# Attention products as plain fp32 on both row halves of TensorE, in place of split fp32r parts on 128 rows

## The reference

```
xn  = (x - mean(x)) * rsqrt(var(x) + eps) * gamma + beta        # per sample
q   = Wq @ xn + bq ;  k, v = Wkv @ ctx + bkv                    # 8 heads x 64 channels
att = softmax((q * scale)^T (k * scale))                        # 256 x 256 per head
out = x + Wo @ (att @ v^T)^T + bo
```

## Time and profile before

| | |
|---|---|
| runs, median | 944.0 us (944.0 and 944.01) |
| profiled execution | 944.01 us, the slower of the two; its span from first to last instruction is 941.7 us |
| PE matmul busy | 919.0 us, 98% |
| PE weight load | 691.6 us, 73% |
| DVE | 810.3 us, 86% |
| ACT | 758.3 us, 81% |
| POOL | 671.0 us, 71% |
| DMA | 93.32 MB, mean 99 GB/s |

### The profile page before, as it was taken

The page is one execution under the profiler, slowest core; times in us unless marked ns, Lnnn a source line. Parts: engine busy times, 40 slices in busy tenths (PEclk is TensorE's granted clock), DMA queues, the critical chain, the costliest instruction groups (busy, mean ns, idle before and its releaser), DMA issues.

```text
span 941.7 us, 25082 instructions
## 1 busy us (share of the span) xinstructions
PE 919.0 (98%) x6852; PEld 691.6 (73%) x6852; DVE 810.3 (86%) x1899; ACT 758.3 (81%) x2569; POOL 671.0 (71%) x648
## 2 busy tenths in 40 slices
PE   5999999999999999999999999999999999999998
PEld 4777777777777777777777777777777777777775
DVE  5888889888889888898888898888898888898885
ACT  2788888788888878887888887888888888888785
POOL 2667777667787667877777776677776677777674
PEclk9999999999999999999999999999999999999999
DMA  6444444444444344444444444434444444433431
GB/s 120 100 107 95 114 100 100 96 106 93 107 110 95 91 109 100 95 117 94 95 100 106 100 105 97 104 89 115 103 100 93 106 96 103 114 90 83 96 82 36
DMA packets 72741, 93.32 MB, mean 99 GB/s; under 512 B 15316, under 2 KB 39892, under 8 KB 72724
## 3 DMA queue, kind: packets, MB, share of 16 engines
q1 hardware_dynamic: 70800, 92.72, 42.6%
q10 hardware_dynamic: 1924, 0.40, 0.3%
HBM read 21.76 MB, written 4.19 MB: 28 GB/s over the span
## 4 chain that ended last, share of the span: by engine, by line
PE 53%; DVE 24%; issue 13%; ACT 9%; DMA 0%; DVEq 0%; ACTq 0%; SPq 0%; POOL 0%
PE turned L488 15%; PE out_bank L502 14%; ACT probs L595 8%; PE fill L457 7%; PE fill L458 7%; DVE xhat L722 5%; DVE neg_max L676 5%; DVE probs_t L671 4%; PE misc L518 3%; PE misc L519 3%; DVE c_straight L730 2%; DVE c_crossed L731 2%; PE fill L463 2%; PE fill L464 2%; DVE t_low L687 2%
## 5 line engine op out<-in xcount | busy, mean ns | idle before, releaser
L788 POOL TENSOR_TENSOR probs<-probs,recip 128x512 f32<-128x512 f32 x512 | 526.6, 1055 | 155.6 <-DVE recip L682 150.0
L595 ACT ACTIVATE probs<-fill,neg_max 128x256 f32<-128x256 f32 x1024 | 475.4, 484 | 82.5 <-DVE neg_max L676 82.5
L676 DVE TENSOR_REDUCE neg_max<-fill 128x2 f32<-128x512 f32 x512 | 347.9, 680 | 65.4 <-PE fill L458 60.7
L488 PE MATMUL turned<-ident,probs 128*128 128x128 f32 x2048 | 325.5, 282 | 6.2 <-DVE probs_t L671 6.2
L457 PE MATMUL fill<-c_straight,t_stack 128*128 128x256 f32 x1024 | 308.9, 324 | 0.5 <-DMA t_stack<-t_low 0.5
L488 PEld LDWEIGHTS turned<-ident,probs 128*128 128x128 f32 x2048 | 224.0, 142 | 114.9 <-issue 62.6
L502 PE MATMUL out_bank<-probs_t,values 128*64 128x256 f32 x2048 | 277.5, 392 | 1.4 <-ACT probs_t L586 1.4
L458 PE MATMUL fill<-c_crossed,t_stack 128*128 128x256 f32 x1024 | 265.2, 280 | 0.0
L595 ACT ACTIVATION_READ_ACCUMULATOR probs<-fill,neg_max 128x1 f32 x1024 | 218.8, 214 | 0.0
L586 ACT COPY probs_t<-turned 128x512 f32<-128x512 f32 x256 | 150.1, 586 | 78.2 <-PE turned L488 77.9
L502 PEld LDWEIGHTS out_bank<-probs_t,values 128*64 128x64 f32 x2048 | 124.4, 136 | 105.7 <-issue 34.8
(11 more groups left out here) (61 smaller groups left out, 547.7 us busy)
## 6 DMA issues: line engine op xcount, KB each, us to landing
t_stack<-t_up SPq DMA_DIRECT2D x256, 128.0 KB, 2.3
t_stack<-t_low SPq DMA_DIRECT2D x256, 128.0 KB, 2.3
x<-in_x SPq DMA_DIRECT2D x64, 128.0 KB, 2.7
c<-in_ctx SPq DMA_DIRECT2D x64, 128.0 KB, 2.7
x_res<-in_x SPq DMA_DIRECT2D x32, 128.0 KB, 2.1
out<-y SPq DMA_DIRECT2D x32, 128.0 KB, 1.7
wq<-in_L_xattn_Wq ACTq DMA_DIRECT2D x2, 128.0 KB
wv<-in_L_xattn_Wkv SPq DMA_DIRECT2D x2, 128.0 KB
```

Source lines behind the costliest of these rows:

```text
L488: mm = pe.transpose(turned[unit % PT_BANKS][:, S * kt + 128 * qt:S * kt + 128 * qt + 128], probs[:, unit % PROBS, qt, 128 * kt:128 * kt + ...
L595: ins = act.activation(probs[:, unit % PROBS, qt, :], bank[:, K * qt:K * qt + K], ACT.Exp, bias=neg_max[:, unit, qt:qt + 1], accum_out=den ...
L676: dve.tensor_reduce(neg_max[:, unit, :], fill[bank_of("scores", unit)][:, :].rearrange("p (t k) -> p t k", t=QT), AX.X, ALU.max, negate=Tr ...
L788: pool.tensor_tensor(p, p, recip[:, unit, :].unsqueeze(2).broadcast_to([128, QT, K]), ALU.mult).then_inc(probs_ready, 1)
```

## The change

The three split products become plain fp32 products with 64 rows, issued two at a time: one on rows 0 to 63 and one on rows 64 to 127 of the array, each into a bank of its own. Nothing is split any more: `t_up`, `t_low`, `t_stack`, `x_stack`, `c_straight`, `c_crossed`, their casts and subtractions and the sixteen stacking DMAs of a pair are gone. Weights, xhat and ctx already lie on both halves.

- A score **step** now makes two units, the even and the odd head of one sample; 8 steps a pair. A projection makes four heads (2 a pair, the banks read by ACT as `t_even` and by DVE as `t_odd`), a values item one half of the keys of both samples (2 a pair, one ACT copy of 1024 columns).
- The `fill` banks are now two **bank pairs**. Values use them too, so `FILLS` has 12 items, and each waits for the readers of the item two places earlier.
- An attend covers two heads, 4 a pair. Unit order is now sample-major within a head pair.
- All positions are new.

```diff
-FILL_BANKS = 4
+FILL_PAIRS = 2
-PROJ, VALUES, DISTANCE = -8.57, -4.16, 1.87
-PE_ORDER = (every("scores", -3.69, UNITS) + every("proj", PROJ, HP, 4) + every("turn", 1.26, UNITS)
-            + every("attend", 4.1, H, PS) + every("values", VALUES, PS * KT, DISTANCE)
+STEPS = UNITS // 2
+SCORES, PROJ, VALUES = -3.7, -8.5, -5.6
+PE_ORDER = (every("scores", SCORES, STEPS, 2) + [(PROJ, "proj", 0), (PROJ + 4.9, "proj", 1)] + every("turn", 1.26, UNITS)
+            + every("attend", 6.1, HP, 4) + every("values", VALUES, KT, 4)
             + [(-13.42, "mean", 0), (-11.99, "var", 0)])
-ACT_ORDER = (every("t_hi", PROJ + 0.21, HP, 4) + every("exp", -2.39, UNITS)
+ACT_ORDER = ([(PROJ + 0.4, "t_even", 0), (PROJ + 5.4, "t_even", 1)] + every("exp", -2.39, UNITS)
              + [work for work in every("copy", 1.27, UNITS) if work[2] not in DVE_EVACS]
-             + every("values", VALUES + 0.38, PS * KT, DISTANCE))
-DVE_ORDER = (every("t_lo", PROJ + 1.08, HP, 4) + every("max", -3.24, UNITS) + every("recip", -1.98, UNITS)
+             + [(VALUES + 1.1, "values", 0), (VALUES + 5.0, "values", 1)])
+DVE_ORDER = ([(PROJ + 0.6, "t_odd", 0), (PROJ + 5.6, "t_odd", 1)] + every("max", -3.24, UNITS) + every("recip", -1.98, UNITS)
              + [work for work in every("copy", 0.93, UNITS) if work[2] in DVE_EVACS]
              + [(-15.75, "moments", 0), (-14.01, "mean_var", 0), (-13.2, "spread", 0),
-                (-12.47, "sample_var", 0), (-11.46, "norm", 0), (-7.73, "c_hi", 0), (18.63, "result", 0)])
+                (-12.47, "sample_var", 0), (-11.46, "norm", 0), (20.63, "result", 0)])
...
-FILLS = [(_kind, _item, _at) for _at, _kind, _item in in_order(PE_ORDER) if _kind in ("scores", "proj")]
+FILLS = [(_kind, _item, _at) for _at, _kind, _item in in_order(PE_ORDER) if _kind in ("scores", "proj", "values")]
...
+            def free_banks(pair, k):
+                for back in range(FILL_PAIRS, NFILL + 1, FILL_PAIRS):
+                    kind, item, step = FILLS[(k - back) % NFILL]
+                    owner = pair.shift(-(back > k) - int(step // UNITS))
+                    if owner.exists():
+                        if kind == "scores":
+                            wait(pe, exp_ready, owner.count(UNITS, 2 * item + 2))
+                        elif kind == "proj":
+                            wait(pe, t_even_ready, owner.count(HP // 2, item + 1))
+                            wait(pe, t_odd_ready, owner.count(HP // 2, item + 1))
+                        else:
+                            wait(pe, values_ready, owner.count(KT, item + 1))
+                        break
+
+            def scores(pair, step, banks):
+                hp, s, p = step // PS, step % PS, pair.parity()
                 for qt in range(QT):
-                    lhs = t_stack[:, h, s, 128 * qt:128 * qt + 128]
-                    dst = bank[:, K * qt:K * qt + K]
-                    pe.matmul(dst, lhs, c_straight[p][:, s, :], start=True, stop=False)
-                    mm = pe.matmul(dst, lhs, c_crossed[p][:, s, :], start=False, stop=True)
+                    for o in range(2):
+                        r = 64 * o
+                        mm = pe.matmul(banks[:, o, K * qt:K * qt + K], t[r:r + 64, hp, s, 128 * qt:128 * qt + 128],
+                                       c2[p][r:r + 64, s, :], start=True, stop=True)
                 mm.then_inc(scored, 1)
...
+            def project(pair, i, banks):
+                for o in range(2):
+                    r = 64 * o
+                    hp = 2 * i + o
+                    mm = pe.matmul(banks[:, o, :], qk_gamma[r:r + 64, 2 * hp:2 * hp + 2, :],
+                                   xhat[pair.parity()][r:r + 64, :, :], start=True, stop=True)
+                mm.then_inc(projected, 1)
+
+            def make_values(pair, kt, banks):
+                for s in range(PS):
+                    r = 64 * s
+                    mm = pe.matmul(banks[:, s, :], c2[pair.parity()][r:r + 64, s, 128 * kt:128 * kt + 128],
+                                   u_t[r:r + 64, :, :], start=True, stop=True)
+                mm.then_inc(values_summed, 1)
...
-            def attend(pair, h):
+            def attend(pair, hp):
...
+                if hp == 0:
+                    wait(pe, values_ready, pair.count(KT, KT))
                     wait(pe, y_ready, pair.count(1, 0))
+                for h in (2 * hp, 2 * hp + 1):
+                    for kt in range(KT):
+                        for s in range(PS):
+                            mm = pe.matmul(out_bank[64 * s:64 * s + 64, 0:S], values[pair.parity()][:, s, kt, h, :],
+                                           probs_t[:, unit_of(h, s) % PROBS_T, kt, :],
+                                           start=(h == 0 and kt == 0), stop=(h == H - 1 and kt == KT - 1))
...
             def exponentials(pair, unit):
-                bank = fill[bank_of("scores", unit)]
+                bank = fill[banks_of("scores", unit // 2)][:, unit % 2, :]
...
+            def copy_values(pair, kt):
+                wait(act, values_summed, pair.count(KT, kt + 1))
...
+                act.copy(values[pair.parity()][:, :, kt, :, :], fill[banks_of("values", kt)][:, :, :]
+                         ).then_inc(values_ready, 1)
```

More of the change, by code:

```diff
@@ L246, in build @@
         y = [sb(f"y_{i}", [128, S]) for i in range(2)]
-        fill = [pb(f"fill_{i}", [128, 512]) for i in range(FILL_BANKS)]
+        fill = [pb(f"fill_{i}", [128, 2, 512]) for i in range(FILL_PAIRS)]
         turned = [pb(f"turned_{i}", [128, 512]) for i in range(PT_BANKS)]
@@ L437, in output_value_products @@
                 mm.then_inc(w_mm, 1)
[L439 to L450, removed]
@@ L467, in fill_bank, with fill_banks @@
+            def make_values(pair, kt, banks):
[4 more added lines that the diff above has]
+                mm.then_inc(values_summed, 1)
+            def fill_banks(pair, kind, item, owner):
                 k = fill_of(kind, item)
-                free_bank(pair, k)
+                free_banks(pair, k)
+                banks = fill[k % FILL_PAIRS]
@@ L469, in fill_bank @@
                 if kind == "scores":
+                    if item % (2 * PS) == 0:
+                        wait(pe, t_even_ready, owner.count(HP // 2, item // (2 * PS) + 1))
+                        wait(pe, t_odd_ready, owner.count(HP // 2, item // (2 * PS) + 1))
+                    scores(owner, item, banks)
+                elif kind == "proj":
                     if item == 0:
[L471 to L473 removed]
@@ L474, in fill_bank @@
-                    scores(owner, item, fill[k % FILL_BANKS])
+                        wait(pe, xhat_ready, owner.count(2, 2))
+                    project(owner, item, banks)
                 else:
                     if item == 0:
-                        wait(pe, x_stack_ready, owner.count(1, 1))
-                    project(owner, item, fill[k % FILL_BANKS])
+                        wait(pe, c_loaded[owner.parity()], owner.dma_count(1) * 2)
+                        if owner.first():
+                            pe.wait_ge(w_act, 7)
@@ L480, in turn_probs @@
+                    make_values(owner, item, banks)
             def turn_probs(pair, unit):
@@ L490, in turn_probs @@
                 mm.then_inc(probs_turned, 1)
-            def attend(pair, h):
-                units = [PS * h + s for s in range(PS)]
-                for unit in units:
+            def attend(pair, hp):
+                for unit in (4 * hp + 2, 4 * hp + 3):
                     probs_t_wait(pe, pair, unit)
-                if h == 0:
-                    wait(pe, values_ready, pair.count(PS * KT, PS * KT))
+                if hp == 0:
+                    wait(pe, values_ready, pair.count(KT, KT))
@@ L499, in attend @@
                     wait(pe, y_ready, pair.count(1, 0))
[L500 to L504, removed]
-                mm.then_inc(attended, 1)
[L507 to L516, removed]
-                lhs = c_straight[pair.parity()][:, s, 128 * kt:128 * kt + 128]
-                pe.matmul(misc[:, :], lhs, u_straight[:, :, :], start=True, stop=False)
-                pe.matmul(misc[:, :], lhs, u_crossed[:, :, :], start=False, stop=True).then_inc(values_summed, 1)
+                for h in (2 * hp, 2 * hp + 1):
[4 more added lines that the diff above has]
+                                           start=(h == 0 and kt == 0), stop=(h == H - 1 and kt == KT - 1))
@@ L533, in steps @@
                 for kind, item, owner in work(pair, PE_ORDER):
-                    if kind == "proj" and owner.first():
-                        if item == 0:
+                    if owner.first() and item == 0:
+                        if kind == "proj":
                             query_key_products()
-                        elif item == 1:
+                        elif kind == "values":
                             output_value_products()
-                    if kind in ("scores", "proj"):
-                        fill_bank(pair, kind, item, owner)
```

(8 more changed lines are left out.)

182 lines of the change are left out of this document (51 added, 131 removed).

## The result

The changed kernel takes **1424.8 us** against 944.0 (median of 2 runs each): 1.510 times as long, 95% interval 1.507 to 1.513. The profiled execution has a span of 1422.9 us.

What follows compares the result with a forecast made beforehand. The hand-over of bank pairs was to bound the kernel, PE, DVE and ACT working in turn. Slots A to H sum to 40.1 us a pair; 76 + 1163 (29 pairs) + 69 gives span 1308, so 1310 us, range 1180 to 1430.

Steps and rivals of the forecast that it cites:

- low clock: Rival: PE's standstills lower its clock, nearly doubling its blocks; 1750 us, or 1450 in part of the slots; chance 0.05.
- A: Slot from score step 2 to the next step: PE work alone, with an attend and transposes, 4.10 us.
- B: Slot from score step 3: scores, maximum, DVE's spread, then PE's variance product and transposes, 3.25 us.
- C: Slot from score step 4: norm and result precede DVE's next maximum, and attend 0 waits for result, 5.39 us.
- D: Slot from score step 5: gated projection 0, transposes of unit 7, ACT's copy and exponentials of unit 11, 4.95 us.
- E: Slot from score step 6: PE work alone, with an attend and transposes, 4.10 us.
- F: Slot from score step 7: gated values 0, then ACT's values copy, two exponentials and a copy in turn, 6.23 us.
- G: Slot from score step 0: projection 1, transposes, attend, then ACT's copy 13 ahead of exponentials 1, 6.65 us.
- H: Slot from score step 1: values 1, then ACT's values copy, exponentials, copy 15 and exponentials 3, 5.43 us.
- PE stays the bound: Rival: ACT gets ahead and fills wait little, 959 us, or 875 with row blocks free of drains; chance 0.07.
- the halves take turns: Rival: the array's row halves do not overlap, each step and item 0.88 us longer, 1610 us; chance 0.04.
- Part of the gates bite: Rival: some of slots F, G, H overlap, 33 to 36 us a pair, 1090 to 1180 us; chance 0.06.

Runs made afterwards that it cites:

- e1: The changed kernel plus eight constant fp32 products on PE before step 0 and before step 2 of each pair, filling its two long waits: 1334.2 us.
- e5: The changed kernel with the order changes of e2 and e4 together: 1094.9 us, 1.160 times the kernel before.
- e2: The changed kernel reordered: a step's two maxima adjacent on DVE, its two exponentials adjacent on ACT, copies after them: 1177.2 us.
- e3: The changed kernel with three bank pairs in place of two, one turned bank in place of two, same order of work: 1161.5 us.
- e7: e1 with both products of a score step on one row half, so the result is not the reference's: 1578.8 us.
- e8: The kernel before with only attends over two heads, 4 a pair in place of 8: 931.6 us, ratio 0.987.
- e9: e8 with the attend one unit later, position 6.35 in place of 6.1: 955.2 us, 1.012 times the kernel before.
- e4: The changed kernel with DVE's result ahead of norm, order only: 1343.1 us.

## Why the prediction was right, and what it missed

**The direction and the mechanism of the bank hand-over held, and the time lies in the range, 1425 of 1180 to 1430, at its very edge.** That it lies inside at all is partly luck. The case as forecast, 1310 with its own range 1205 to 1385, holds the 1334 of the kernel at full clock (e1), but not the 1425; the widening to 1430 was for unknown costs and happens to cover 91 us of low clock, for which the prediction had a rival of its own at 1450. One of its signs of being wrong came true as well: the period is 43.8, over 43. Of its other signs, PE's share is 75% (about 72% was forecast), and the four waits for exponentials are 1.68, 2.41, 1.67 and 2.41 us (1.5 to 2.5). Slots in us, means over 28 pairs from the starts of the score records; e1 is the changed kernel at full clock:

| slot | forecast | after | e1 | e5 |
|---|---|---|---|---|
| A | 4.10 | 5.74 | 4.11 | 4.11 |
| B | 3.25 | 3.26 | 3.26 | 3.26 |
| C | 5.39 | 5.80 | 5.80 | 4.12 |
| D | 4.95 | 5.13 | 5.14 | 4.28 |
| E | 4.10 | 4.12 | 4.12 | 4.12 |
| F | 6.23 | 6.34 | 6.34 | 3.89 |
| G | 6.65 | 7.98 | 6.72 | 5.50 |
| H | 5.43 | 5.42 | 5.43 | 3.89 |
| sum | 40.1 | 43.8 | 40.9 | 33.2 |

- **PE's own work**: right where it decides a slot, short in the sum. A and E are PE blocks alone, 4.10 against 4.11 and 4.12, so a step and an attend cost what was taken from the earlier trace rows, with the full 0.30 for their edges. In e5, at full clock, PE is busy 866.5 us over 29 pairs (the view by stretches, from 71.2 to 1033.2), 29.9 a pair; the forecast was 28.7. Before it was 28.3, against 28.1 in the prediction's sum. So PE's own work grew by 1.6 a pair and not by 0.6; which blocks hold the difference was not taken apart.
- **Hand-over of banks**: right, by e2 and e3. D, F, G and H are within 0.2 at full clock. e5 against e1, both at full clock, puts a price on the order as a whole, result included: 239 us.
- **Result behind norm**: right in kind, C 0.41 short. Norm's two instructions took 2.07 us where the earlier trace rows have 1.64. This is the largest error at full clock.
- **The work that left DVE, ACT, POOL and DMA** was worth nothing, as said.
- **The step that failed is the clock.** The prediction made it a rival with a chance of 0.05 and priced "in part of the slots" at 1450; it is part of the main case. G and A lose 1.3 and 1.6 us a pair, 91 us by e1, and these are most of the 115 between 1310 and 1425. The other 24 are the 0.8 a pair that the slots were short. The prediction had worked out waits of up to 2.6 us, and then gave the clock little chance; the full mean clock that it names is that of a kernel which has no such waits. That a block at the low level takes nearly twice as long was about right: here a step takes 1.85 to 1.98 in place of 1.14, and a projection 1.92 in place of 1.02. The rows that it read this from, 0.59 against 0.23 in the earlier trace rows, show 2.6 times, more than a clock at half its rate would make.
- **PE stays the bound**, **the halves take turns**: fell, by the ring of waits and by e7. **Part of the gates bite**: fell, all of them do.
- Even with the order mended, e5 is 1.16 times the kernel before. It needs 33.2 a pair, of which PE is busy 29.9. The other 3.3 are waits. Before the steps that end D, F and H PE waits 2.4 in all: from a step to the release of its banks pass 3.8 us, and PE has about 3 to do. In B it waits 0.5 for DVE's spread, and in G 0.3 for the values copy ahead of the projection.

## What to carry to other kernels

When buffers are merged into larger ones, ask at each place who must be done before the next user may start, and whether that reader stands before or behind it in its own engine's list; the time from fill to release, with everything that is queued in between, is the floor of that slot. Count the time in which PE would stand still, and cost the blocks behind it at the lower clock too, instead of giving this to a rival. A block of products in another array layout was costed at 0.30 us for its edges, so fewer and longer blocks should pay by themselves. They did, but gave 12.6 us of the 37 expected (e8), and with the attend one unit's scores later the gain was lost (e9): the other engines' lists must still cover the longer block.

## What was not expected of the hardware

- **Waits of about 2.4 us were enough for the clock to fall, but not each time.** In the changed kernel slot G ran low in 22 of 28 pairs and A in all; in e4, with the same 2.40 us ahead of step 0, G ran low in 2 of 28. So the length of the last wait alone does not decide; what else does is open. Filling both waits with products of constants kept the clock up (e1, 0.999 on the mean).
- **Norm on DVE ends with GpSimd's divisions.** The same instruction, 128 x 256:

```profile
L661 DVE TENSOR_SCALAR xhat<-x,mean,rstd x64: 409/1072/1126, 9.4 to 1355.7; 128x256 f32<-128x256 f32 x64
```

The line's view gives min, median and max in ns; before, the median was 590 and the extremes 407 and 1127. Here the timeline has the two norm instructions of a pair from 652.79 on for 2.07 us and two divisions beside them from 652.62 on for 2.08. Before, the divisions began 0.60 ahead of norm and here 0.17, and the first of its two instructions took 0.59 before and 1.02 here. The first pair has no division beside its two norm instructions, for there are no scores yet: they take 0.41 us each, the shortest of the run, here and before. In both traces each of the other 62 ends 0.15 behind the end of a division. So norm's time goes with where it meets POOL's divisions. That DVE stands still and waits for POOL, rather than running slower, is argued; no run took the divisions away from the later pairs.
